# Weight loads moved to SyncE's queue, in a two-layer attention kernel whose parts are put in a new order

## The reference

```
x = x + _L0_xattn_ref(_layernorm(x, axis=-1), ctx_512, ctx_512)
x = x + _L0_ffn_ref(_layernorm(x, axis=-1), ...)
x = x + _L1_xattn_ref(_layernorm(x, axis=-1), ctx_512, L1_xattn_Wq, L1_xattn_Wkv_expand, L1_xattn_Wout)
x = x + _L1_ffn_ref(_layernorm(x, axis=-1), L1_ffn_w1, L1_ffn_w2)
```

## Time and profile before

| | |
|---|---|
| median of 3 runs (lowest, highest) | 555.26 us (550.74, 555.32) |
| the profiled execution, its span | 557.25 us, 555.4 us |
| PE busy, of the span | 500.6 us, 90% |
| DVE, ACT, POOL busy | 66%, 65%, 51% |
| mean granted TensorE clock | 0.974 of full speed |
| moved by DMA | 43.99 MB, mean 79 GB/s |

### The profile page before, as it was taken

One profiled execution on the slowest core, in us unless ns is written; L12 is line 12 of the kernel. 1 busy time (PEld: TensorE's weight loads), 2 busy tenths in 40 slices (PEclk: granted clock), 3 DMA queues, 4 the chain that ended last, 5 costly groups with the idle time before them and its releaser, 6 DMA issues.

```text
span 555.4 us, 10890 instructions
## 1 busy us (share of the span) xinstructions
PE 500.6 (90%) x3863; PEld 320.6 (58%) x3878; DVE 369.2 (66%) x818; ACT 358.7 (65%) x705; POOL 282.7 (51%) x535
## 2 busy tenths in 40 slices
...
GB/s 201 246 266 110 212 98 30 74 34 72 45 98 99 34 70 34 121 74 46 83 25 113 31 73 41 74 82 38 45 69 88 44 67 39 61 63 116 21 11 19
DMA packets 66542, 43.99 MB, mean 79 GB/s; under 512 B 36712, under 2 KB 61160, under 8 KB 66488
## 3 DMA queue, kind: packets, MB, share of 16 engines
...
...
## 4 chain that ended last, share of the span: by engine, by line
PE 60%; ACT 11%; DVE 10%; DMA 7%; POOL 4%; SPq 3%; issue 3%; POOLq 0%; ACTq 0%
PE banks L662 15%; PE banks L697 9%; PE banks L641 4%; DMA parts_qA<-QP 2%; PE banks L688 2%; PE banks L614 2%; PE banks L599 2%; PE banks L753 2%; PE banks L629 2%; PE banks L649 2%; PE banks L762 2%; PE banks L718 2%; PE banks L733 2%; PE banks L738 2%; PE banks L812 2%
## 5 line engine op out<-in xcount | busy, mean ns | idle before, releaser
L1228 DVE TENSOR_REDUCE neg_maxA<-banks 128x8 f32<-128x1024 f32 x64 | 75.8, 1210 | 33.1 <-PE banks L614 33.1
L902 ACT ACTIVATE PA<-banks 128x1024 f32<-128x1024 f32 x64 | 63.1, 1032 | 14.0 <-PE banks L629 13.8
L1130 POOL TENSOR_TENSOR vB<-vB,route_c 128x512 f32<-128x512 f32 x32 | 34.2, 1070 | 72.9 <-DVE vB L1287 72.9
L926 ACT ACTIVATE tB<-banks,route_half 128x128 f32<-128x128 f32 x128 | 36.6, 370 | 48.1 <-PE banks L662 45.1
L697 PE MATMUL banks<-w2T,hTB 128*128 128x256 f32 x288 | 66.1, 384 | 0.1
L662 PE MATMUL banks<-w1T,xTB 128*128 128x512 f32 x128 | 60.7, 597 | 0.0
L662 PE MATMUL banks<-w3T,xTB 128*128 128x512 f32 x128 | 60.1, 592 | 0.0
L697 PEld LDWEIGHTS banks<-w2T,hTB 128*128 128x128 f32 x288 | 53.4, 190 | 10.3 <-ACT hTB L939 2.1
L1138 POOL TENSOR_SCALAR_AFFINE_SELECT PC<-PC 128x1024 f32<-128x1024 f32 x32 | 35.1, 1097 | 26.0 <-ACT PC L902 26.0
L1228 DVE TENSOR_REDUCE neg_maxC<-banks 128x8 f32<-128x1024 f32 x32 | 38.5, 1217 | 7.2 <-PE banks L738 6.9
L662 PEld LDWEIGHTS banks<-w3T,xTB 128*128 128x128 f32 x128 | 24.3, 190 | 30.6 <-issue 30.6
...
## 6 DMA issues: line engine op xcount, KB each, us to landing
...
```

The costliest lines, as they stand in the source:

```text
L902: return op(dst[:, 8 * j:8 * (j + 1), :], ps[:].rearrange("p (h t) -> p h t", t=P), ACT.Exp, scale=scale).then_inc(S[name], 1)
L926: ins = op(tB[:, (e0 + i) * HID:(e0 + i + 1) * HID], ps[:, i * HID:(i + 1) * HID], ACT.Tanh, scale=rt["half"][:, e0 + i:e0 + i + 1])
L1130: g.tensor_tensor(hB[:, sl].rearrange("p (e h) -> p e h", e=4), vB[:, sl].rearrange("p (e h) -> p e h", e=4), rt["c"][:, e0:e0 + 4].unsque ...
L1228: v.tensor_reduce(dst[:, 8 * j:8 * (j + 1)], ps[:].rearrange("p (h t) -> p h t", t=P), FREE, ALU.max, negate=True).then_inc(S[name], 1)
```

## The change

Part W leaves ScalarE's list and stands in SyncE's; its functions move with it and are otherwise unchanged. PROGRAMS is written anew for all five engines, so the order of nearly everything changes, on each engine. FILL has 58 dummy matmuls for 62. No computation is added or removed.

On SyncE at the start, before: x tile 1 and two more tiles, then the keys' write and the first queries' restack.

```diff
     "sync": """
-        X/2 X/3 K/0 A1/0 C0/0 C0/1 A1r/0 V/0 A1/1 V/1 A1r/1 X/4 X/5 A1/2 A3/0 K/1 S2/0 A1/3 Kr/1 A3/1 A1r/2 X/6 C2.1/0
+        W.3/0 W.6/0 K/0 A1/0 A1/1 A1r/0 C0/0 C0/1 A1r/1 X/2 W.2/0 W.0/0 X/3 W.1/0 W.4/0 W.5/0 W.7/0 V/0 V/1 A3/0 S2/0
...
     "scalar": """
-        W.1/0 W.0/0 A0/0 A1/0 W.2/0 A0/1 A1/1 Kr/0 W.3/0 A0/2 W.6/0 W.5/0 W.4/0 A1/2 W.7/0 A0/3 A3/0 S1.0/0 S1.1/0 A1/3
+        A0/0 A1/0 A0/1 A1/1 Kr/0 A0/2 A3/0 A1/2 S1.0/0 S1.1/0 A4.0/0 A4.1/0 A4.2/0 A4.3/0 A3/1 C2.1/0 C2.1/1 A5.0/0
...
 FILL = """
-    A2.0/0:20 A3/0:8 A2.0/1:3 D4/11:4 C5/15:6 C9/14:4 D4/13:3 D1/15:6 D3/14:8
+    A2.0/0:20 S1.0/0:8 C6.0/14:8 C9/14:4 D1/15:6 D2/15:3 D3/14:9
...
+            def up_half(i):
+                for w, name in zip(w_ab, ("w1T", "w3T")):
+                    for c in range(DC):
+                        sp.dma_start(w[:, c, i * BANK:(i + 1) * BANK].rearrange("p (q n) -> p q n", n=D),
+                                      a[name][4 * c + 2 * i:4 * c + 2 * i + 2].rearrange("q p n -> p q n")).then_inc(w_in[f"up{i}"], 16)
+
+            def W(s, t, u, j):
+                if j == 0:
+                    sp.wait_ge(S["ksrc_in"], 16)
+                    in_rows(f1, "f1T").then_inc(w_in["D1"], 16)
...
-            walk(act, "scalar", {"W": W, "Kr": Kr, "S1": S1, "S2": S2, "A1": A1, "A3": A3, "A4": A4, "A5": A5, "B1": B1, "B2": B2, "B3": B3, "B4": B4, "B5": B5,
+            walk(act, "scalar", {"Kr": Kr, "S1": S1, "S2": S2, "A1": A1, "A3": A3, "A4": A4, "A5": A5, "B1": B1, "B2": B2, "B3": B3, "B4": B4, "B5": B5,
```

More of the change, by code:

```diff
@@ L91 @@
[L91 to L95, removed]
@@ L106 @@
[L106 to L110, removed]
@@ L111 @@
[L111 to L120, removed]
@@ new lines @@
+        B5.2/2@2 B2/3@0 B3/3@6 C1/1@2 A5.0/4@3 A5.1/4@0 C2.0/1@1 A6.0/4@0 A6.1/4@2 C5/0@3 A2.1/5@4 A2.2/5@6 A2.3/5@0
+        B6/2@3 C6.0/0@0 C6.1/0@4 B5.0/3@2 B4/3@6 C4.0/1@0 C7/0@2 C4.1/1@4 C1/2@0 C8/0@1 C2.1/2@2 A2.0/6@6 A1/8@0
+        B5.1/3@3 C5/1@1 A2.1/6@4 C2.0/2@2 A2.2/6@0 A2.3/6@6 A3/5@3 C9/0@4 B5.2/3@2 B1/4@3 C6.0/1@4 C6.1/1@0 B6/3@2
+        A4.0/5@0 C7/1@3 A4.1/5@4 A4.2/5@0 A4.3/5@6 C8/1@2 C10/0@3 C4.0/2@4 C4.1/2@0 C1/3@2 B2/4@6 B3/4@4 B4/4@0 C5/2@2
+        C2.1/3@3 B5.0/4@4 B5.1/4@5 A3/6@6 A5.0/5@7 A5.1/5@3 A2.0/7@0 A1/9@2 A6.0/5@4 A6.1/5@3 B5.2/4@5 A2.1/7@0
@@ new lines @@
+        D2/7@4 A3/13@3 C9/8@6 B5.2/11@7 A5.0/12@0 A5.1/12@1 C6.1/9@4 B6/11@3 C4.0/10@4 A4.0/13@0 C7/9@3 A6.0/12@2
+        A4.1/13@0 A4.2/13@4 A6.1/12@3 C8/9@2 C1/11@7 C4.1/10@0 A2.0/14@2 A4.3/13@4 C10/8@6 A2.1/14@0 A2.2/14@4
+        A5.0/13@7 A5.1/13@6 A2.3/14@2 A6.0/13@7 B1/12@0 C9/9@1 C2.0/11@6 B2/12@0 B3/12@4 B4/12@2 B5.0/12@0 C10/9@1
+        B5.1/12@4 D1/8@5 D3/7@0 A3/14@6 C2.1/11@7 D2/8@2 A2.0/15@0 A2.1/15@5 C5/10@7 B5.2/12@4 D4/7@7 A4.0/14@2
+        A6.1/13@4 A4.1/14@0 B6/12@7 A4.2/14@2 A4.3/14@0 C4.0/11@4 C6.0/10@2 C6.1/10@6 A5.0/14@0 A5.1/14@1 D1/9@2
```

273 lines of the change are left out of this document (137 added, 136 removed).

## The result

The changed kernel takes 559.11 us (median of 20 runs, 553.28 to 565.49), the one before 555.29 us beside it (20 runs): a ratio of 1.0061, 95% interval 1.0038 to 1.0084. It is slower by 3.4 us (2.1 to 4.7), where 7 us less was forecast. The profiled execution has a span of 558.0 us (before 555.4).

What follows compares the result with a forecast made beforehand. The prediction took TensorE's own list of work (busy 500.6 of 555.4 us) as the bound. Start -6 and A4/0 to B1/0 -1 sum to -7: 550.25 beside the profiled 557.25, 548.3 beside the median; range 542 to 559.

Steps and rivals of the forecast that it cites:

- Start, -6.0: Start of the kernel: tile 0's second scores (A4/0) begin at 37.5 us against 43.52, a gain of 6.0 us.
- just hidden: At the start: tile 0's maxima rows, behind 2.9 MB of weights, land by 29 to 34 us, or 37 with one hold-up.
- The ring rival: Tile 0's first restack is held behind weights in the queue, A4/0 at 42.1: -1.4 - 1, 552.9 us; chance 12%.
- the warm start: TensorE stays at full clock at the start, A4/0 near 34: -9.5 - 1, 544.8 us; chance 10%.
- A4/0 to B1/0, -1: From tile 0's second scores to B1/0, 17.9 us before: 1 us gained, bounds -2 to +3.
- the 53 that I named: Sign at the start: TensorE's B1/0 would begin near 53 us.
- Middle.* Same matmuls, another order: **0: Middle of the kernel: no change in time from the new order, bounds -3 to the slower rival.
- Restacks too close to their readers: Too little work between C2.0 and C4.0 at tiles 1, 2, 13, 14, and A1 and A2.0 at 11: +15.7, 564.0; 20%.
- my own line: Sign in the middle: forecast wrong if TensorE's waits for KC, QC or QA pass 7 us.
- End, 0: From C2.0/15 to the end: 4.8 us more work ahead, C4.0/15 6.4 earlier; net 0, bounds -1.5 to +4.8.
- The end is rigid: The 56.8 us from C2.0/15 to the end are all latency, so 4.8 us are given back: 553.1; chance 16%.
- Dummies, 0: Dummy matmuls, 58 for 62, all stand in waits: no change in time.

Runs made afterwards that it cites:

- the mended seam: Changed kernel's order to 86 us with C0/0 late on ScalarE, then the earlier kernel's order, with A2/4 and C0/1 moved ahead on GpSimd: 547.68 us, 0.9903.
- The reverse crossing: The kernel before, with weights on ScalarE, up to A5.1/2 on TensorE, then the changed kernel's order and dummies: 564.24 us, 1.0187 against the kernel before.
- the three swaps: Changed kernel with three ready transfers moved ahead on SyncE in the middle, and C0/0 late on ScalarE: 556.75 us, 1.0028 against the kernel before.
- C0/0 late: Changed kernel with tile 0's third normalisation moved behind tile 2's two output copies on ScalarE: 558.19 us, 1.0069 against the kernel before.

## Why the prediction was wrong

- **Start, -6.0: right.** Tile 0's scores at 19.86 (19.6), tile 1's at 23.79 (23.1), A4/0 at 36.90 (37.5): -6.6. SyncE read tile 0's queries back from 14.89 (14.6), behind tile 1's write, a wait that was in the sum. S1 didn't wait for f1T. That A4/0 came so close is in part luck: S1's first matmuls took 1.88 us, at the full clock, where I had priced 3.78, and A4/0 then waited 0.77 us for tile 0's maxima rows, which I had called just hidden. The ring rival is out, and so is the warm start.
- **A4/0 to B1/0, -1: off by a little.** The stretch took 18.3 us (17.9 before), 0.4 more and not 1 less, inside the bounds. B1/0 came at 55.17; the 53 that I named doesn't follow from my own terms, which give 54.4 (37.5 + 17.9 - 1).
- **The step that failed: behind B1/0 the sum goes over to "*Middle.* Same matmuls, another order: **0**".** I had written that "the same work now meets TensorE sooner" and had bounded that for 43 to 61 us only; from 61 to 100, where VectorE and GpSimd were as busy, and over the 400 us of the middle, I priced the new order at nothing. It measured, by the lead, 4.6 us lost from 80 to 100 and some 4 from 320 to 420. That the new rest and not the early start is the cost is shown by the mended seam: with the same early start, the old rest is 1.6% better than the new one (0.9903 for 1.0061), the edits at the seam included. The reverse crossing (+1.9%) shows the restack waits with the old start, but most of its time can be its own seam.
- **"Restacks too close to their readers": the right mechanism at the wrong size.** Waits for restacked tiles rose from 1.6 to 6.2 us, and my own line for it was 7. Tile 2 (2.3) and tile 11 (1.4, the keys of its block C) carried them, and the maxima rows (2.2), which I hadn't looked at; tiles 1, 13 and 14 cost under 0.5 each. What decides is less the work between C2.0 and C4.0 than what stands ahead of the transfer on SyncE, as the three swaps showed (6.2 to 1.4 us of waits).
- **End, 0: right within its bounds.** C2.0/15 to the end is 4.4 us shorter, against 4.8 later in the list, and by the lead 1 us was lost. "The end is rigid" is out.
- **Dummies, 0, and the clock: not priced.** The mean granted clock is 0.972 against 0.977; 0.005 of 557 us is at most 2.8 us, of a difference of 3.4 to 3.8. In the profile the half clock at 88 to 96 us follows the wait for ScalarE; the mended seam lost wait and half clock together.

What is left open: how much of the loss from 85 to 100 us is one wait (C0/0 late moved it by ten microseconds), which engine's list one would have to change in the new rest besides SyncE's, and what the new rest costs behind the old start without a wait at the seam.
